# A mixture-of-experts and attention block on one core: the first expert pass split into three groups of batches instead of two

## Chip, core and metric

One NeuronCore of a Trainium2 chip (trn2) runs the whole kernel. Times are device microseconds of an execution; lower is better.

## What is computed

The input is `x` of shape (4, 1024, 128): four batches of 1024 tokens. The output is three residual steps in a row, all in float32:

```python
x = x + 0.5 * ffn(layernorm(x))
x = x + attention(layernorm(x))      # differential attention, two softmaxes per row
x = x + 0.5 * ffn(layernorm(x))

def ffn(t):                          # top 2 of 8 experts
    logits = t @ Wr.T + br
    top_v, top_i = top_k(logits, 2);  w = softmax(top_v)
    o_e = relu(t @ W1[e].T + b1[e]) @ W2[e].T + b2[e]       # 128 -> 512 -> 128
    return layer_norm(t + sum_k w_k * o_{top_i[k]}) * gamma + beta
```

## The kernel before

Each engine runs one instruction stream written out by hand, and semaphores order them. The work comes in five stages: a prologue, the first expert pass, attention over the four batches, the second expert pass, and an end.

**Prologue.** The four batches of `x` are loaded and normalised. For each batch TensorE turns the rows (`turn_rows`) and multiplies them by the router (`logits`); VectorE reads the logits and picks two experts for each token (`read_logits`, `choose`), TensorE counts (`prefix`), and VectorE works out for every token and choice a row number in a table of rows in DRAM (`place`). The three are called `route`. GpSimd then sends the normalised rows there by indirect transfers (`scatter`), 16 a batch of 128 rows each, so that the rows of one expert lie together. Between the routes TensorE turns the weights of the eight experts (`weights`), with VectorE and ScalarE copying them out of PSUM, and at the end the product of the attention's projections (`M`) is formed.

**Groups and tiles.** Batches 0 and 1 are group 0, batches 2 and 3 are group 1. When a group is placed, VectorE makes its table (`table`): the running row counts per expert (`carry`) tell how many tiles of 128 rows each expert has, and which expert and rows each tile takes. A group of two batches has 2 x 2048 / 128 + 7 = 39 tiles (`GSLOTS`), since each of eight experts may end in a tile that is not full; a pass has 78 (`SLOTS`). SyncE writes padding behind the rows of each expert (`pad`, eight a group) and waits in `group_ready` for the table, the pads and the row transfers of the group. Then it loads one tile after another into a ring of 16 buffers (`load`).

**A tile.** In `step` TensorE transposes the rows of tile s + 2 (`turn_x`, L946), multiplies tile s + 1 by the first weights (`first`, L953) and tile s by the second (`second`, L963). ScalarE copies and applies the first half of the relu, VectorE the rest (L1357) and adds the last bias (`add_b2`, L1365). In the first pass SyncE writes the result y back to DRAM (`write_y`, L357), 12 iterations behind its loads in group 0 and 7 behind in group 1. In the same loop GpSimd sends the rows of batches 2 and 3, one transfer a tile, in steps 0 to 31. From step `GATHER_AT` = 40 on it gathers the results of batches 0 and 1 (L478), and VectorE merges them into `x` in small pieces (`MERGE_AT` = 49, `MERGING`). The normalised `xn` of batch 0 is turned at steps `XN_AT` = 74 and 77. SyncE issues the pads of group 1 in its iterations 16 to 23.

**What follows.** Attention begins when the pass is over. During attention the results of batches 2 and 3 are gathered, and batches 0 to 2 are routed for the second pass. In the second pass batch 3 is routed between the tiles, a few VectorE instructions a step (`CHOOSE_AT` = 11), and GpSimd sends results and rows.

The order in the prologue before: VectorE does route 0, the weights, route 1, table 0, route 2, the copy of the projections, route 3, table 1 and `Mh`/`Ml`; then the steps begin, and TensorE waits for all four batches to be placed and for both tables. GpSimd sends batches 0 and 1 back to back (L465).

Of the kernel before, what the change touches and what calls it, by code (L numbers as in the profile page):

```python
# [29 lines left out]
def macaron_kernel(nc, x_in, w_q12, w_k12, w_v, lq1, lk1, lq2, lk2, Wr, br, W1, b1, W2, b2, gamma, beta, out):  # L30
# [9 lines left out]
    GN = GB * S  # L40
    REGION = GN + P
    ROW = D + 1
    GSLOTS = 2 * GN // P + E - 1
    SLOTS = 2 * GSLOTS
# [6 lines left out]
    assert D == P and S == TB * P and F % P == 0 and SLOTS % 2 == 0 and FC % 2 == 0 and TB % QG == 0  # L51

    rows = [nc.dram_tensor(f"rows{g}", [E * REGION + P, ROW], F32).ap() for g in range(2)]
    yrows = [nc.dram_tensor(f"yrows{g}", [GSLOTS * P, D], F32).ap() for g in range(2)]
# [3 lines left out]
    with ctx:  # L58
# [45 lines left out]
        carry, base = sb("carry", E), sb("base", E)  # L104
        carry_i = sb("carry_i", 2 * E, I32)

        GT = GN // P
        tile128 = sb("tile128", GT)
        ntile, tend, onesE = sb("ntile", E), sb("tend", E, parts=1), sb("onesE", E, parts=1)
        shift = sb("shift", 2 * E)  # L110
        sidx = sb("sidx", GSLOTS, parts=1)

        block_at = sb("block_at", SLOTS, I32, parts=1)
        row_of = sb("row_of", SLOTS, I32, parts=1)
# [37 lines left out]
        cmp2 = lent_z(GSLOTS * E)  # L152
        assert at[0] <= ATT
        eidf, offf, roff = lent_z(GSLOTS), lent_z(GSLOTS), lent_z(GSLOTS)
# [35 lines left out]
        rows_sent = [sem(f"rows_sent{par}") for par in range(2)]  # L190
# [13 lines left out]
        def route_bank(a):  # L204

            return 5 if a < BATCHES and a % 2 else 7
# [21 lines left out]
        def y_at(T):  # L228

            return bank((6, 1)[T % 2], 0, D)  # L230

# [35 lines left out]
        def y_gone(T):  # L267

            r = T % RING
            return (y_written[r], sent(T, r)) if T - RING < SLOTS else (y_sent[r], sent(T, r) - sent(SLOTS, r))  # L270
# [4 lines left out]
        BETA_AT = 18  # L275
        FIND_AT = (8, GSLOTS + 1)
        GATHER_AT = GSLOTS + 1
# [4 lines left out]
        XN_AT = SLOTS - 4  # L282
        ROWS_AT = 16
        LAST_AT, LAST_BY = GSLOTS + 9, 9
# [32 lines left out]
        def _(sp):  # L317
# [13 lines left out]
            for g in range(2):  # L331
                sp.dma_start(rows[g][E * REGION:, :], padrows[:, :]).then_inc(pads_sent, 16)
# [5 lines left out]
            def group_ready(p, g):  # L338
                sp.wait_ge(table_ready, 2 * p + g + 1)
                sp.wait_ge(pads_sent, 16 * (2 + E * (2 * p + g + 1)))  # L340
                for par in range(2):
                    sp.wait_ge(rows_sent[par], 16 * PAIRS * (2 * p + g + 1))

            def load(p, s):
                T, g = SLOTS * p + s, s // GSLOTS
# [8 lines left out]
            def write_y(s):  # L354
                r = s % RING
                wait_apart(sp, (y_sb, s + 1))
                sp.dma_start(yrows[s // GSLOTS][s % GSLOTS * P:(s % GSLOTS + 1) * P, :], ys[:, r * D:(r + 1) * D]).then_inc(y_written[r], 16)  # L357

            def all_sent(g):
                for r in range(RING):  # L360
                    sp.wait_ge(y_sent[r], sent(SLOTS + GSLOTS * (g + 1), r) - sent(SLOTS, r))

            def pads(p, g):
                sp.wait_ge(counts_ready, 2 * p + g + 1)
                for e in range(E):
                    pad(g, e)
# [4 lines left out]
            for s in range(SLOTS):  # L371
                if s == RING:
                    sp.wait_ge(counts_ready, 2)
                if RING <= s < RING + E:
                    pad(1, s - RING)
                if s == GSLOTS:
                    for t in range(s - Y_BEHIND, s - Y_NEAR):
                        write_y(t)
                    group_ready(0, 1)
                load(0, s)  # L380
                if Y_BEHIND <= s < GSLOTS:
                    write_y(s - Y_BEHIND)
                if s >= GSLOTS:
                    write_y(s - Y_NEAR)
            for s in range(SLOTS - Y_NEAR, SLOTS):
# [5 lines left out]
            for s in range(SLOTS):  # L391
                if s == 30:
                    sp.wait_ge(counts_ready, 4)
                if 30 <= s < 30 + E:
                    pad(1, s - 30)
                if s == GSLOTS:
                    group_ready(1, 1)
                load(1, s)
                if s == GSLOTS + RING - 1:
# [22 lines left out]
        def _(pool):  # L422
# [14 lines left out]
            steps.then(pool.iota(sidx[:, :], [[1, GSLOTS]], base=0, channel_multiplier=0, allow_small_or_imprecise_dtypes=True))  # L437
# [21 lines left out]
            def scatter(p, b, pieces=range(2 * TB)):  # L459
# [3 lines left out]
                for i in pieces:  # L463
                    j, k = i // 2, i % 2
                    pool.indirect_dma_start(rows[b // GB], bass.IndirectOffsetOnAxis(slot_v[:, b, j, k:k + 1], 0),  # L465
                                            rows_of(p, b)[:, j, k, :], None).then_inc(rows_sent[b % 2], 16)

            def gather(b, pieces):

                for i in pieces:  # L470
# [7 lines left out]
                    pool.indirect_dma_start(z[:, i * D:(i + 1) * D], None, yrows[b // GB],  # L478
                                            bass.IndirectOffsetOnAxis(slot[:, b * PAIRS + i:b * PAIRS + i + 1], 0)).then_inc(loaded, 16)

            def all_written(g):
                for r in range(RING):
                    wait_apart(pool, (y_written[r], sent(GSLOTS * (g + 1), r)))

            def send(s):
                T = SLOTS + s
# [17 lines left out]
            for b in range(GB):  # L504
                scatter(0, b)
            for s in range(SLOTS):
# [4 lines left out]
                if s == GATHER_AT:  # L511
                    all_written(0)
                if GATHER_AT <= s < GATHER_AT + PAIRS:
                    i = s - GATHER_AT
                    gather(0, range(i, i + 1))
                if GATHER_AT + PAIRS <= s < GATHER_AT + 2 * PAIRS:
                    i = s - GATHER_AT - PAIRS
                    gather(1, range(i, i + 1))
# [3 lines left out]
            all_written(1)  # L522
# [44 lines left out]
            for s in range(SLOTS):  # L567
# [13 lines left out]
        def _(act):  # L581
# [17 lines left out]
            def make_rows(p, b, n, tiles=range(TB)):  # L599

                if p:

                    act.wait_ge(rows_sent[b % 2], 16 * PAIRS * (BATCHES // 2 + b // 2))
# [47 lines left out]
            def step(p, s):  # L651
                t = SLOTS * p + s
                if s + 2 < SLOTS:
# [3 lines left out]
                if 0 <= s + 1 < SLOTS:  # L657
# [51 lines left out]
            def attention(b, n):  # L709
# [17 lines left out]
                for i in range(TB):  # L727
                    if last and not after and i == 6:
                        copy_tgtT(a, 0)
                    if b == 0 and i == 0:  # L730
                        for r in range(RING):
                            act.wait_ge(y_written[r], sent(SLOTS, r))
# [76 lines left out]
            for b in range(BATCHES):  # L809
# [9 lines left out]
                if b:  # L819
# [7 lines left out]
            act.wait_ge(table_ready, 2)  # L827
            for s in range(-2, SLOTS):
                step(0, s)
                if MERGE_AT + 23 <= s < MERGE_AT + 27:  # L830
# [12 lines left out]
            for s in range(-2, SLOTS):  # L843
# [10 lines left out]
                if s == GSLOTS - 1:  # L854
                    act.wait_ge(table_ready, 4)
# [26 lines left out]
        def _(pe):  # L882
# [40 lines left out]
            def logits(a):  # L923
                pe.wait_ge(tgtT_sb, 2 * a + 2)
                if a >= BATCHES:
                    pe.wait_ge(slots_ready, a)
                elif a >= 2:
                    pe.wait_ge(slots_ready, a - 1)
# [39 lines left out]
            def step(p, s):  # L968
                t = SLOTS * p + s
                if s + 2 < SLOTS:  # L970
                    turn_x(t + 2)
                    w_at[s + 2] = expert_offset(PE, s + 2)
                if 0 <= s + 1 < SLOTS:
# [21 lines left out]
            def multiply_M(b):  # L995
                pe.wait_ge(xnTh_sb, b + 2)
                pe.wait_ge(xnTl_sb, b + 2)
                for m in range(4):
                    if b:
                        pe.wait_ge(p_ready, 2 * TB * b - 1 + m // 2)  # L1000
                    elif m == 1:
                        pe.wait_ge(y_sb, SLOTS)
# [100 lines left out]
            for b in range(BATCHES):  # L1103
                turned = b + 1 == BATCHES
                if b and not turned:
# [7 lines left out]
                if not turned:  # L1113
# [19 lines left out]
            for s in range(-2, SLOTS):  # L1133
                step(0, s)
                if s in (XN_AT, XN_AT + 3):
# [5 lines left out]
            pe.wait_ge(table_ready, 3)  # L1141
            for s in range(-2, SLOTS):
# [629 lines left out]
```

## Time and profile before

| | |
|---|---|
| timed runs | 677.21 us, median of 3 (676.9 to 678.15) |
| span of the profiled execution | 746.1 us (its own time is not given apart from the span) |
| TensorE, matmul | busy 595.6 us, 80% of the span |
| VectorE / ScalarE / GpSimd | 61% / 59% / 51% |
| TensorE's mean granted clock | 0.908 |

The span is from the first to the last instruction of the execution that was recorded, and it is 69 us longer than a timed run. Busy shares are means over stages that differ; the views further down are read by stage.

### The profile page before, as it was taken

The page shows a single profiled execution, that of the slowest core. Times are in us where ns is not written, and L with a number is a line of the kernel's source. Part 1 is how long each engine was busy: PE and PEld are TensorE (multiplying, and loading weights), DVE is VectorE, ACT ScalarE, POOL GpSimd, SP SyncE. Part 2 cuts the span into 40 slices and gives each one's busy share as a digit, 9 for nine tenths or more (in the row PEclk, how much of TensorE's full clock was granted, in tenths as well). Part 3 has the DMA queues.
Part 4 walks back from the last instruction along what each step waited for, and adds up shares of the span by engine and source line. Part 5 has one row for each costly group of instructions (what it writes and reads, how often), then busy time and mean ns, then how long its engine had stood idle before and what let it go on. Part 6 is the DMA issues. An engine that isn't in the chain of part 4 may idle for free.

```text
span 746.1 us, 16949 instructions
## 1 busy us (share of the span) xinstructions
PE 595.6 (80%) x4276; PEld 544.6 (73%) x4276; DVE 454.9 (61%) x1432; ACT 443.2 (59%) x1144; POOL 380.9 (51%) x475
## 2 busy tenths in 40 slices
PE   2626189999999879899898998969288479999955
PEld 1625079999998768787886897858187479999821
DVE  5527445654667788799688789655035236457636
ACT  4434056666665677678786866837054236786744
POOL 6345225541445277568324575835745645545633
PEclk9965579999999999999999999989679679999969
DMA  8412124443333111010000000212221222522042
GB/s 278 141 38 65 50 60 102 110 104 84 98 98 90 51 29 29 8 30 22 1 1 1 23 30 15 69 29 63 57 58 54 69 74 54 175 64 59 28 147 84
DMA packets 54253, 49.22 MB, mean 66 GB/s; under 512 B 9926, under 2 KB 45938, under 8 KB 53904
## 3 DMA queue, kind: packets, MB, share of 16 engines
q1 hardware_dynamic: 45312, 31.25, 15.0%
q0 software_dynamic: 8640, 16.87, 7.3%
q8 instruction: 39, 0.64, 0.4%
q14 instruction: 54, 0.44, 0.2%
q10 hardware_dynamic: 208, 0.02, 0.0%
HBM read 25.99 MB, written 23.02 MB: 66 GB/s over the span
## 4 chain that ended last, share of the span: by engine, by line
PE 51%; DVE 19%; issue 9%; another core or an unknown queue 7%; POOL 6%; ACT 6%; DMA 1%; ACTq 1%; DVEq 0%; POOLq 0%; SPq 0%
PE banks L953 17%; PE banks L963 16%; DVE nb L1607 4%; PE banks L946 3%; PE banks L1050 3%; DVE scratch L1614 2%; PE banks L885 2%; PE banks L887 2%; PE banks L886 2%; POOL zb L478 1%; POOL rs L455 1%; ACT scratch L639 1%; POOL rows L465 1%; DVE st_r L1217 1%
## 5 line engine op out<-in xcount | busy, mean ns | idle before, releaser
L963 PE MATMUL banks<-blocks,scratch 128*128 x1248 | 172.8, 283 | 24.6 <-issue 21.9
L963 PEld LDWEIGHTS banks<-blocks,scratch 128*128 128x128 f32 x1248 | 158.3, 199 | 26.8 <-issue 26.7
L953 PE MATMUL banks<-scratch 128*128 128x128 f32 x1248 | 173.4, 284 | 4.3 <-ACT scratch L639 3.0
L1357 DVE TENSOR_SCALAR scratch<-banks,blocks 128x128 f32<-128x128 f32 x312 | 95.2, 347 | 120.5 <-PE banks L953 68.8
L953 PEld LDWEIGHTS banks<-scratch 128*128 128x128 f32 x1248 | 157.9, 198 | 9.4 <-issue 9.2
L465 POOL DMA_INDIRECT rows<-rowbuf,slot x96 | 100.1, 1043 | 55.6 <-issue 48.6
L633 ACT ACTIVATE scratch<-banks 128x128 f32<-128x128 f32 x156 | 43.3, 277 | 136.0 <-PE banks L946 66.5
L489 POOL DMA_INDIRECT results<-scratch x78 | 79.2, 1015 | 77.0 <-DVE scratch L1365 45.4
L646 ACT ACTIVATE scratch<-banks,blocks 128x128 f32<-128x128 f32 x312 | 96.8, 366 | 14.3 <-remote 6.6
L721 ACT ACTIVATE scratch<-banks,nb 128x1024 f32<-128x1024 f32 x64 | 71.3, 1115 | 45.7 <-DVE nb L1607 45.1
L639 ACT ACTIVATE scratch<-blocks 128x512 f32 x156 | 97.5, 625 | 0.0
L1607 DVE TENSOR_REDUCE nb<-banks 128x1 f32<-128x1024 f32 x64 | 76.6, 1217 | 14.7 <-PE banks L887 12.9
L1365 DVE TENSOR_TENSOR scratch<-banks,blocks 128x128 f32<-128x128 f32 x156 | 45.0, 288 | 53.0 <-PE banks L963 28.7
L478 POOL DMA_INDIRECT zb<-yrows,slot x48 | 51.5, 1073 | 44.0 <-DVE scratch L1365 26.2
L1050 PE MATMUL banks<-xn,scratch 128*128 128x128 f32 x512 | 65.5, 283 | 1.8 <-ACT scratch L707 1.7
L1050 PEld LDWEIGHTS banks<-xn,scratch 128*128 128x128 f32 x512 | 62.4, 199 | 3.1 <-issue 2.4
L885 PE MATMUL banks<-xnTh,xmh 128*128 128x512 f32 x128 | 53.7, 420 | 13.3 <-ACT scratch L721 13.2
L465 POOL DMA_INDIRECT rows<-scratch,slot x32 | 30.6, 957 | 52.7 <-DVE scratch L1365 27.2
L946 PE MATMUL banks<-ident,scratch 128*128 128x128 f32 x156 | 44.4, 285 | 16.2 <-ACT scratch L633 6.8
L887 PE MATMUL banks<-xnTh,xml 128*128 128x512 f32 x128 | 50.9, 397 | 0.0
L886 PE MATMUL banks<-xnTl,xmh 128*128 128x512 f32 x128 | 50.7, 396 | 0.0
L1614 DVE SCALAR_TENSOR_TENSOR scratch<-scratch,cc 128x1024 f32<-128x1024 f32 x32 | 40.9, 1279 | 5.3 <-POOL cc L530 5.3
(210 smaller groups left out, 882.7 us busy)
## 6 DMA issues: line engine op xcount, KB each, us to landing
scratch<-rows SPq DMA_DIRECT2D x156, 64.5 KB
yrows<-scratch SPq DMA_DIRECT2D x78, 64.0 KB
rows<-padrows SPq DMA_DIRECT2D x34, 64.5 KB
x<-in_L_attn_x_dram SPq DMA_DIRECT2D x4, 512.0 KB, 5.6
scratch<-in_L_ffn_W_dram SPq DMA_DIRECT2D x1, 2048.0 KB, 19.3
rows<-rowbuf,slot POOLq DMA_INDIRECT x96
results<-scratch POOLq DMA_INDIRECT x78
zb<-results SPq DMA_DIRECT2D x1, 1024.0 KB
```

Source lines behind the costliest of these rows:

```text
L465: pool.indirect_dma_start(rows[b // GB], bass.IndirectOffsetOnAxis(slot_v[:, b, j, k:k + 1], 0), rows_of(p, b)[:, j, k, :], None).then_inc ...
L489: pool.indirect_dma_start(results, bass.IndirectOffsetOnAxis(xt_v[:, r, D:ROW].bitcast(I32), 0), ys[:, r * D:(r + 1) * D], None, bounds_ch ...
L639: act.activation(staged(T, 0, FC), blocks[:, bass.ds(at, F)], ACT.Copy).then_inc(w1_sb, 1)
L646: ins = act.activation(hT_of(T, c), hT_at(T, c), ACT.Relu, bias=blocks[:, B1_AT + c:][:, bass.ds(at, 1)], scale=1.0)
L721: act.activation(pp, banks[:, 2 * m * 512:(2 * m + 2) * 512], ACT.Exp, bias=nb[:, 2 * i + m:2 * i + m + 1], scale=1.0, accum_out=ll[:, i:i ...
L885: pe.matmul(o, ah, bh, start=True, stop=False)
L946: pe.transpose(bank(0, 0, P), xt_v[:, r, 0:D], ident[:, :]).then_inc(xT_ps, 1)
L953: ins = pe.matmul(hT_at(T, c), staged(T, c), xT_of(T), start=True, stop=True)
L963: ins = pe.matmul(y_at(T), hT_of(T, c), blocks[:, W2_AT + c * D:][:, bass.ds(at, D)], start=(c == 0), stop=(c == FC - 1))
L1050: ins = pe.matmul(bank(6, 0, D), dT[t % 2][:, k * P:(k + 1) * P], vb[:, k * D:(k + 1) * D], start=(k == 0), stop=(k == TB - 1))
L1357: ins = dve.tensor_scalar(hT_of(T, c), hT_at(T, c), blocks[:, B1_AT + c:][:, bass.ds(at, 1)], 0.0, ALU.add, ALU.max)
L1607: dve.tensor_reduce(nb[:, c], banks[:, 2 * m * 512:(2 * m + 2) * 512], AX_X, ALU.max, negate=True).then_inc(nb_ready, 1)
```

## The change

- The first pass has three groups: batch 0, batch 1, and batches 2 and 3 (`MEMBERS`). A group of one batch has 23 tiles, so the pass has 23 + 23 + 39 = 85 (`SLOTS[0]`), the second pass still 39 + 39 = 78. Every use of `GSLOTS`, `SLOTS` and `b // GB` becomes a look-up by pass and group (`START`, `TILES`, `group_of`, `group_at`, `whole_group`, `FIRST_T`). There are three row tables and three y tables in DRAM, a semaphore `rows_sent` for each batch and a `carry` for each group.
- VectorE makes table 0 right behind route 0, ahead of the weights. Batch 3 is no longer routed in the prologue: TensorE makes its logits behind the product M, VectorE chooses in steps 0 to 2 and places in steps 4 to 6, and tables 1 and 2 are made in steps 8 to 19, a piece a step.
- TensorE and ScalarE wait for a group's table when they come to its first tile, and no longer for everything ahead of the pass.
- GpSimd sends batch 0 and four transfers of batch 1 ahead of the tiles, with a pause (`rest`) behind each: two memsets of 8 columns, each waited for. The other 44 go with the tiles, five in four steps up to step 16 and one a step after it, until step 39.
- SyncE's pads for group 1 go with iterations 15 to 22, for group 2 with 38 to 45. y is written 12 iterations behind the loads in all groups; at the start of a group five writes go ahead at once and the next five iterations write none.
- `FIND_AT`, `BETA_AT` and `XN_AT` move; `GATHER_AT` stays at step 40 and `MERGE_AT` at 49.

```diff
+    MEMBERS = [[range(0, 1), range(1, 2), range(2, 4)], [range(0, 2), range(2, 4)]]
+    TILES = [[2 * TB * len(members) + E - 1 for members in groups] for groups in MEMBERS]
+    START = [[sum(tiles[:g]) for g in range(len(tiles))] for tiles in TILES]
+    SLOTS = [sum(tiles) for tiles in TILES]
...
-        BETA_AT = 18
-        FIND_AT = (8, GSLOTS + 1)
-        GATHER_AT = GSLOTS + 1
+        BETA_AT = 28
+        AHEAD, DENSE = 4, 16
+        CHOOSE_FIRST, PLACE_FIRST, TABLE_FIRST = 0, 4, 8
+        FIND_AT = (20, 24, 34, 47)
+        GATHER_AT = 40
...
+        def first_sends(s):
+            return AHEAD + min(s, DENSE) * 5 // 4 + max(s - DENSE, 0)
...
             def group_ready(p, g):
-                sp.wait_ge(table_ready, 2 * p + g + 1)
-                sp.wait_ge(pads_sent, 16 * (2 + E * (2 * p + g + 1)))
-                for par in range(2):
-                    sp.wait_ge(rows_sent[par], 16 * PAIRS * (2 * p + g + 1))
+                sp.wait_ge(table_ready, whole_group(p, g))
+                sp.wait_ge(pads_sent, 16 * (len(rows) + E * whole_group(p, g)))
+                for b in MEMBERS[p][g]:
+                    sp.wait_ge(rows_sent[b], 16 * PAIRS * (p + 1))
...
-            for s in range(SLOTS):
-                if s == RING:
-                    sp.wait_ge(counts_ready, 2)
-                if RING <= s < RING + E:
-                    pad(1, s - RING)
-                if s == GSLOTS:
+            for s in range(SLOTS[0]):
+                for g in range(1, NGROUPS[0]):
+                    e = s - (START[0][g] - E)
+                    if e == 0:
+                        sp.wait_ge(counts_ready, whole_group(0, g))
+                    if 0 <= e < E:
+                        pad(g, e)
+                if s in START[0][1:]:
                     for t in range(s - Y_BEHIND, s - Y_NEAR):
                         write_y(t)
-                    group_ready(0, 1)
+                    group_ready(0, group_at(0, s))
                 load(0, s)
-                if Y_BEHIND <= s < GSLOTS:
+                near = [at for at in START[0][1:] if at <= s < at + Y_BEHIND - Y_NEAR]
+                if s >= Y_BEHIND and not near:
                     write_y(s - Y_BEHIND)
-                if s >= GSLOTS:
-                    write_y(s - Y_NEAR)
...
-            for b in range(GB):
-                scatter(0, b)
-            for s in range(SLOTS):
+            def rest():
+                for _ in range(2):
+                    steps.then(pool.memset(idle[:, :], 0.0))
+            for i in range(PAIRS):
+                scatter(0, 0, range(i, i + 1))
+                rest()
+            for i in range(AHEAD):
+                scatter(0, 1, range(i, i + 1))
+                rest()
+            for s in range(SLOTS[0]):
                 wait_apart(pool, (y_sb, s + 1))
-                if s < 2 * PAIRS:
-                    i = s % PAIRS
-                    scatter(0, GB + s // PAIRS, range(i, i + 1))
+                for k in range(first_sends(s), min(first_sends(s + 1), 3 * PAIRS)):
+                    i = k % PAIRS
+                    scatter(0, 1 + k // PAIRS, range(i, i + 1))
...
+            logits(BATCHES - 1)
             pe.wait_ge(M_sb, 1)
-            pe.wait_ge(slots_ready, BATCHES)
-            pe.wait_ge(table_ready, 2)
-            for s in range(-2, SLOTS):
+            for s in range(-2, SLOTS[0]):
                 step(0, s)
+                if s == CHOOSE_FIRST + 3:
+                    prefix(BATCHES - 1)
...
-            for b in range(BATCHES):
+            for b in range(BATCHES - 1):
                 route(0, b)
                 if b == 0:
+                    at_once(table(0, 0))
                     small_weights()
                     weights(range(E))
-                if b == 1:
-                    at_once(table(0))
...
-            for s in range(-2, SLOTS + 1):
+            choosing, placing = choose(BATCHES - 1), place(BATCHES - 1, BATCHES - 1)
+            tabling = itertools.chain(table(0, 1), table(0, 2))
+            for s in range(-2, SLOTS[0] + 1):
                 step(0, s)
+                if s == CHOOSE_FIRST:
+                    read_logits(BATCHES - 1)
+                if CHOOSE_FIRST <= s < CHOOSE_FIRST + 3:
+                    next(choosing, None)
+                    next(choosing, None)
+                if PLACE_FIRST <= s < PLACE_FIRST + 3:
+                    next(placing, None)
+                    next(placing, None)
+                if TABLE_FIRST <= s < TABLE_FIRST + 12:
+                    next(tabling, None)
```

## Rows read from the trace of the kernel before

**Rows 1.** The page: span, and the granted clock in 40 slices.
```profile
span 746.1 us, 16949 instructions
...
PEclk9965579999999999999999999989679679999969
```

**Rows 2.** Windows: busy us (x instructions) of each engine, clock, DMA share, GB/s.
```profile
97.00:187.00 90.00, 88.49 (x766) 88.06 (x766) 45.74 (x152) 60.40 (x184) 33.53 (x35) 0.97 0.36 94
518.00:616.00 98.00, 63.24 (x430) 59.36 (x429) 29.77 (x115) 37.25 (x109) 55.79 (x57) 0.76 0.22 62
```

**Rows 3.** The chain that ended last, 30 to 90 us: start, us, what.
```profile
41.34 6.36 another core or an unknown queue
...
72.49 11.24 another core or an unknown queue
```

**Rows 4.** Timeline of GpSimd: start us, us, instruction, idle before it.
```profile
2.69 0.29 POOL L438 TENSOR_SCALAR_AFFINE_SELECT ident<-ident 128x128 f32<-128x128 f32 x1 [0.16 <-POOL sidx L437]
...
29.09 1.24 POOL L465 DMA_INDIRECT rows<-rowbuf,slot  x1 [11.11 <-issue]
...
60.79 1.19 POOL L465 DMA_INDIRECT rows<-rowbuf,slot  x1 [11.52 <-issue]
...
80.00 0.96 POOL L465 DMA_INDIRECT rows<-rowbuf,slot  x1 [0.30 <-issue]
...
146.46 0.96 POOL L465 DMA_INDIRECT rows<-scratch,slot  x1 [0.94 <-issue]
...
271.81 2.06 POOL L478 DMA_INDIRECT zb<-yrows,slot  x1 [0.17 <-issue]
...
285.51 1.08 POOL L478 DMA_INDIRECT zb<-yrows,slot  x1 [0.17 <-issue]
```

**Rows 5.** Timeline of VectorE, same columns.
```profile
29.90 0.69 DVE L1201 COPY blocks<-banks 128x512 f32<-128x512 f32 x1 [1.42 <-PE banks L907]
...
52.07 0.23 DVE L1243 TENSOR_TENSOR lg<-banks,brb 128x64 f32<-128x64 f32 x1 [3.65 <-remote]
...
59.48 0.17 DVE L1309 CAST carry_i<-carry 128x8 int32<-128x8 f32 x1
...
63.87 0.22 DVE L1243 TENSOR_TENSOR lg<-banks,brb 128x64 f32<-128x64 f32 x1
...
71.42 0.15 DVE L1206 TENSOR_TENSOR nlam<-lame 128x1 f32<-128x1 f32 x1
```

**Rows 6.** Timeline of SyncE's queue; some rows merge several issues (x).
```profile
84.19 13.49 SPq L352 DMA_DIRECT2D scratch<-rows  x13
...
110.73 0.20 SPq L336 DMA_DIRECT2D rows<-padrows  x1
...
132.44 0.02 SPq L352 DMA_DIRECT2D scratch<-rows  x1
...
159.39 3.50 SPq L357 DMA_DIRECT2D yrows<-scratch  x6
```

**Rows 7.** DMA issues: the nearest transfer with a landing, KB, us to landing.
```profile
out_dram<-x SPq DMA_DIRECT2D x4, 256.0 KB, 2.0
```

**Rows 8.** Timeline of TensorE.
```profile
39.52 1.85 PE L931 MATMUL banks<-wrT,sum_r 128*128 128x8 f32 x16
...
68.58 3.53 PE L931 MATMUL banks<-wrT,sum_r 128*128 128x8 f32 x16
...
88.41 1.17 PE L1128 MATMUL banks<-xn 128*128 128x128 f32 x4
...
96.31 0.47 PE L946 MATMUL banks<-ident,scratch 128*128 128x128 f32 x1 [6.73 <-DVE Ml L1685]
...
249.42 0.30 PE L946 MATMUL banks<-ident,scratch 128*128 128x128 f32 x1 [1.26 <-ACT scratch L633]
```

**Rows 9.** Windows, of the tile transposes (L946) alone: busy us (x count).
```profile
104.05:183.64 79.59, 11.45 (x42) 6.01 (x42) 1.00 0.38 99
554.80:571.65 16.85, 2.24 (x8) 1.19 (x9) 1.00 0.15 45
```

More of the change, by code:

```diff
@@ L50, in macaron_kernel @@
     QG = 4
-    assert D == P and S == TB * P and F % P == 0 and SLOTS % 2 == 0 and FC % 2 == 0 and TB % QG == 0
-    rows = [nc.dram_tensor(f"rows{g}", [E * REGION + P, ROW], F32).ap() for g in range(2)]
-    yrows = [nc.dram_tensor(f"yrows{g}", [GSLOTS * P, D], F32).ap() for g in range(2)]
+    assert D == P and S == TB * P and F % P == 0 and FC % 2 == 0 and TB % QG == 0
+    rows = [nc.dram_tensor(f"rows{g}", [E * REGION + P, ROW], F32).ap() for g in range(max(NGROUPS))]
+    yrows = [nc.dram_tensor(f"yrows{g}", [tiles * P, D], F32).ap() for g, tiles in enumerate(TILES[0])]
     results = nc.dram_tensor("results", [2 * N, D], F32).ap()
@@ L189, in macaron_kernel @@
         xt_loaded = [sem(f"xt_loaded{r}") for r in range(RING)]
-        rows_sent = [sem(f"rows_sent{par}") for par in range(2)]
+        rows_sent = [sem(f"rows_sent{b}") for b in range(BATCHES)]
         went_by = sem("went_by")
@@ L230, in y_at, with group_of, group_at, whole_group @@
             return bank((6, 1)[T % 2], 0, D)
+        def group_of(p, b):
+            return [b in members for members in MEMBERS[p]].index(True)
+        def group_at(p, s):
+            return sum(s >= at for at in START[p]) - 1
+        def whole_group(p, g):
+            return sum(NGROUPS[:p]) + g + 1
+        def carry_of(p, g):
+            at = (whole_group(p, g) - 1) * E
+            return carries[:, at:at + E]
         def rows_of(p, b):
@@ L330, in _ @@
             sp.wait_ge(masks_made, 1)
-            for g in range(2):
+            for g in range(len(rows)):
                 sp.dma_start(rows[g][E * REGION:, :], padrows[:, :]).then_inc(pads_sent, 16)
@@ L566, in _ @@
             scatter(1, BATCHES - 2, range(3, 6))
-            for s in range(SLOTS):
+            for s in range(SLOTS[1]):
                 send(s)
@@ L818, in _ @@
                         copy_tgtT(b + 1, i)
-                if b:
+                if b and following:
                     gap(b)
@@ L842, in _ @@
             b, a = BATCHES - 1, 2 * BATCHES - 1
-            for s in range(-2, SLOTS):
+            for s in range(-2, SLOTS[1]):
                 step(1, s)
@@ L1102, in _ @@
             logits(0)
-            for b in range(BATCHES):
-                turned = b + 1 == BATCHES
-                if b and not turned:
+            for b in range(BATCHES - 1):
+                if b:
                     for i in range(2):
@@ L1112, in _ @@
                     weights(range(E))
-                if not turned:
+                if b + 1 < BATCHES - 1:
                     logits(b + 1)
@@ L1708, in _ @@
             routing = last_route(n)
-            choosing, placing, tabling = choose(a), place(a, BATCHES - 1), table(1)
+            choosing, placing, tabling = choose(a), place(a, BATCHES - 1), table(1, 1)
             ending = [last_sums(b, n + 1 + b) for b in range(GB)]
             adding = [last_add(b) for b in range(GB)]
-            for s in range(-2, SLOTS + 1):
+            for s in range(-2, SLOTS[1] + 1):
                 step(1, s)
```

212 lines of the change are left out of this document (110 added, 102 removed).

## Prediction

> **What bounds the kernel now.** I read the page first. TensorE's granted clock is full nearly everywhere except in slices 3 to 6 of 40, the later prologue, and here and there in slices 27 to 34, the second pass [rows 1]. So between long stretches ruled by TensorE (tiles, attention) lie two weak places, and the windows view prices the second: in a clean stretch of tiles TensorE records 766 matmuls in 90 us, 8.5 in a us; in 518 to 616 us, in the second pass, 430 in 98 us at clock 0.76 [rows 2]. At the clean rate 430 take 50.5 us, so 47.5 us are lost. The chain of waits shows what kind of time the prologue loses: 6.36 and 11.24 us are put down to "an unknown queue" [rows 3]. In the second of them VectorE stands still until 83.75 although the logits that it waits for end at 72.1.
>
> GpSimd's timeline tells when this happens. Its row transfers follow one another every 1.26 us, from 29.09 to 49.27 and from 60.79 to 80.96 us [rows 4]. Both standstills begin 12 us into such a run and end 2.8 us after it (52.07 and 83.75). In the clean tiles a transfer takes 0.96 and the gap to the next 0.94, so one comes every 1.9 us, and nobody stands still. In 518 to 616 us GpSimd has 57 instructions against 35 in the clean 90 us [rows 2].
>
> Now the span against the time. The span is 746.1 us, and the profiled execution's own time is known only by it; the timed runs have a median of 677.21, 69 us less. Clean tiles have no 69 us to give. The second pass can give 47.5, and the prologue about 21, for without standstills it would run so: the weights end some 4 us earlier, batch 1 is routed by 48 us (VectorE takes 7.4 from reading the logits to the slots [rows 5]), before GpSimd is through with batch 0 at 49.3. Sixteen more transfers end at 69.8. SyncE issues the first load 3.2 us after the last transfer, as in the trace (80.96, 84.19 [rows 4, 6]); it lands some 2.0 us later, by the nearest landing [rows 7]: the tiles start at **75.2** instead of 96.3 [rows 8]. VectorE's own road (two more routes, table 1) would be ready at 74. 47.5 + 21.1 = 68.6, and 69 are to be explained. So I take it that the timed runs hardly have these standstills, and that their prologue is bound by the row transfers of batches 0 and 1, one behind the other.
>
> A rule of the Trainium skill speaks against a gain here ("NOTIFIC — the notification-queue block", 7.1 Overflow): the block that records events never loses a record inside, it holds its producers back instead. By that rule the standstills belong to the recording, the timed runs gain nothing from their removal, and the sum below stays. The same page (section 10) says that a record costs the engine nothing, which would put them into the timed runs: the second rival. No row here tells the two apart.
>
> **The change, part by part**, in terms of the timed runs, without standstills.
>
> *The start.* Now batch 0's transfers alone gate the first load. A pause is two tiny memsets, each waited for. One costs about 0.1 us and the 0.16 until the next instruction that GpSimd's waited-for iota shows, and a transfer behind arithmetic starts 0.17 us later and takes 1.08 instead of 0.96 [rows 4]. So transfer and pause take about 1.8 us. The last of 16 ends at 29.09 + 15 x 1.8 + 1.08 = 57.2, and the first load lands at 57.2 + 3.2 + 2.0 = 62.4. Bounds of the spacing are 1.65 (no slower transfer) and 2.7 (every one like the one of 2.06 us [rows 4]): 60 to 76 us.
>
> The other road is VectorE's and TensorE's. VectorE was free for the weights 1.42 us before the copy at 29.90, at 28.5. Now table 0 comes first. Before it took 4.4 us (59.48 to 63.87 [rows 5]) for 39 tiles; for 23 I take 3.8, so 32.3. The first copy slips by 2.4 us, the end of the weights by some 2, to 39. Logits 1 take 1.85 us at the full clock, route 1 takes 7.4 from 41, and ScalarE's exponential for it lies behind the rows of batch 2, about 1.5: 50.0. Logits 2 take 3.53 us at the half clock [rows 8] and are ready at 50.5; route 2 ends at 58.0. Lambda and the copy of the projections take 1.1 (71.42 to 72.49 [rows 3, 5]), their product 1.2: 60.3. Behind it TensorE now does logits 3, 3.53 us at the half clock: **64.0**. Route 3, table 1 and batch 1's transfers are gone from this road. The later of both roads counts, 64.0 against 75.2: **-11.2 us**. With TensorE warm it is 61, and GpSimd's 62.4 counts (-12.8); with the widest pauses 76 (+1).
>
> *Seven more tiles*, 85 for 78. In the clean stretch 42 tile transposes lie in 79.59 us, 1.895 us a tile [rows 9]. **+13.3 us**, and nothing hides it, since TensorE has no gap there.
>
> *Batch 3 routed between tiles*: its 7.4 us on VectorE go over tiles 0 to 6, two tables over tiles 8 to 19. The second pass does just this with its last batch: 8 transposes in 16.85 us there, where 8 clean ones take 15.16, so 1.7 us [rows 9]. The choosing falls into the first, slow tiles: **+1.5**, between 0.5 and 3.4 (twice what the row shows).
>
> *SyncE's queue at the borders.* Iterations 15 to 22 each issue a pad, and iteration 15 waits for counts that VectorE now makes in its step 8; behind it stand loads 15 and on, and the writes of y. An iteration with a pad takes (132.44 - 110.73) / 8 = 2.71 us, a load alone 1.04, a write 0.58 [rows 6]; TensorE eats a tile in 1.9. From step 8 SyncE needs 8 x 2.71 and five writes before load 23, 25.2 us with its waits, and the load lands at 27.2; TensorE wants it 12.4 tiles behind, at 23.6. So it stands for 3.5 us. At border 46 the pads make SyncE late again (between the borders it regains only 0.27 us an iteration), and the last row transfer goes seven tiles ahead instead of eight: 2.7 by the same reckoning. Against it: with SyncE 15% quicker than in the recorded execution both vanish (18.4 + 2.5 + 2.4 is below 23.6). Bounds 0 and 6.2; I take **+3**.
>
> *The rest.* Gathers and merging keep their step numbers while the last tiles come seven later, so the pieces of xn no longer meet the merging. Where they met, tile 76 waited 1.26 us for ScalarE [rows 8]; I take **-1**, between 0, if ScalarE is late there for another reason, and -2.5. The gathers of batches 0 and 1 start at step 40 as before, those of 2 and 3 in attention as before. The new waits of the second pass ask for transfers long done; semaphores, carries and buffers per group lie on no road.
>
> Sum: -11.2 + 13.3 + 1.5 + 3 - 1 = **+5.6 us**, on the median **682.8 us**. The span of 746.1 would besides lose the prologue's 21.
>
> **The rivals.**
>
> 1. *Borders free, TensorE warm*: -12.8 + 13.3 + 0.5 - 1 = 0, so 677. For it: SyncE's iteration is not far over a tile. Against it: the half clock from 45 us on [rows 1]. Chance 0.17.
> 2. *The standstills are in the timed runs too*, the other sign. The pauses bring the transfers to 1.8 us, near the 1.9 at which nobody stands still, and the 21.1 us come on top: 661.7. Half of it: 672. Against it stands the account above: with 21 real us the rest of the trace would have to give 69 and has 48. Five or six real us are possible, and the change gains from 5.6 on. Chance 0.24, mostly near 672.
> 3. *The pauses are dear*: above a spacing of 1.9 us batch 0's transfers decide the start, and each further 0.1 costs 1.5 us; at 2.3 the time is 688. The transfer of 2.06 us speaks for it, the one of 1.08 against. Chance 0.07.
> 4. The forecast, 682.8, with its own range 678.5 to 687: chance 0.52.
>
> **The numbers.** Some 0.2% (1.35 us) can be told from no change. Faster: rival 2 and a part of rival 1, 0.28. Same: most of rival 1, 0.14. Slower: forecast and rival 3, 0.58. The range leaves out the full form of rival 2 and the far end of rival 3: 668 to 689.
>
> **What would show it.** In the profile after: 163 tile transposes; the first near 64 us; batch 0's transfers every 1.8 us and no standstill among them; TensorE waiting near tiles 21 and 44 for loads, SyncE late by its pads. The span should fall by some 15 us while the timed runs don't. A first tile at 64 and timed runs near 665 would prove me wrong on what the standstills are; free borders would take 3 us from the sum.

## The result, and the profile after

The kernel after takes 701.04 us (median of four runs, 700.69 to 703.43), the kernel before beside it 677.68 (676.9 to 679.45): ratio 1.0349, 95% interval 1.0327 to 1.0372, so 23.4 us slower. The forecast was 682.8 us, its range ended at 689. The direction was right, the size a quarter of what came.

The page of after, span and granted clock in 40 slices, to be read against [rows 1]:
```profile
span 701.6 us, 17576 instructions
...
PEclk9975899999999999999999999998999998999969
```
The recorded span falls by 44.5 us while the timed runs rise by 23.4. The weak clock of slices 27 to 34 is gone, and with it the standstills of the second pass, although nothing of that pass was changed but its waits. The window of [rows 2] in after, and then in a second recording of before that is told of below:
```profile
518.00:616.00 98.00, 90.98 (x768) 89.06 (x769) 52.01 (x183) 62.60 (x188) 73.18 (x75) 0.97 0.38 105
518.00:616.00 98.00, 91.09 (x781) 89.69 (x780) 54.63 (x186) 64.95 (x200) 67.38 (x68) 0.97 0.36 105
```
768 matmuls and 75 instructions of GpSimd stand there in after instead of 430 and 57. So the trace of before wasn't typical of its timed runs, and a clean one was made: the kernel before, unchanged, was run and recorded again (run e0). Its page, and one line each of its GpSimd, SyncE and TensorE timelines at the start:
```profile
span 675.5 us, 16949 instructions
...
PEclk9975699999999999999999999997999997999969
```
```profile
69.31 0.96 POOL L465 DMA_INDIRECT rows<-rowbuf,slot  x1 [0.31 <-issue]
```
```profile
72.89 2.59 SPq L352 DMA_DIRECT2D scratch<-rows  x3
```
```profile
75.13 0.45 PE L946 MATMUL banks<-ident,scratch 128*128 128x128 f32 x1 [7.62 <-DMA scratch<-rows]
```
The last row transfer of batches 0 and 1 ends at 70.3, the first load is issued at 72.9 and its landing starts the tiles at 75.13; the prediction had worked out 69.8, 73 and 75.2 for the timed runs. Everything below is read against this trace.

**The start of after.** TensorE, ScalarE and VectorE, one fence each:
```profile
63.71 1.19 PE L1172 MATMUL banks<-xn 128*128 128x128 f32 x4 [4.43 <-DVE xn L1726]
64.70 3.42 PE L974 MATMUL banks<-wrT,sum_r 128*128 128x8 f32 x16
67.97 0.45 PE L989 MATMUL banks<-ident,scratch 128*128 128x128 f32 x1
```
```profile
51.69 0.17 ACT L869 ACTIVATE lame<-banks 128x2 f32<-128x2 f32 x1 [3.99 <-PE banks L1162]
51.76 3.17 ACT L637 ACTIVATE scratch<-x,nm,rs 128x128 f32<-128x128 f32 x8
...
59.06 0.20 ACT L669 ACTIVATE ex<-ex 128x8 f32<-128x8 f32 x1
```
```profile
59.30 0.17 DVE L1315 TENSOR_SCALAR den<-ex 128x8 f32<-128x8 f32 x1 [3.91 <-ACT ex L669]
```
SyncE issues the first loads long before, so they decide nothing:
```profile
55.92 13.49 SPq L381 DMA_DIRECT2D scratch<-rows  x13
```
The road is the one forecast (routes, projections, product, logits 3), but the first tile comes at 67.97 instead of 64.0. ScalarE first waits 3.99 us with lambda's exponential at the head of its queue, then makes the rows of batch 3, and only then takes the exponential of route 2; VectorE stands 3.91 us for it. In before the same order cost nothing, since there the first tile waits 7.62 us for its load (the line at 75.13 above), behind the row transfers.

**The borders.** SyncE's waits and its queue, and the windows of the tile transposes (L989) over eight tiles at border 23 and six at border 46:
```profile
SPq L364 <- DVE carry_i L1356: 10.2, 1, 10.2
```
```profile
80.66 0.33 SPq L388 DMA_DIRECT2D yrows<-scratch  x1
91.88 0.35 SPq L365 DMA_DIRECT2D rows<-padrows  x1
93.06 0.34 SPq L381 DMA_DIRECT2D scratch<-rows  x1
93.52 0.37 SPq L388 DMA_DIRECT2D yrows<-scratch  x1
94.65 0.34 SPq L365 DMA_DIRECT2D rows<-padrows  x1
...
112.24 0.34 SPq L365 DMA_DIRECT2D rows<-padrows  x1
113.39 0.34 SPq L381 DMA_DIRECT2D scratch<-rows  x1
113.85 3.42 SPq L388 DMA_DIRECT2D yrows<-scratch  x6
118.19 6.55 SPq L381 DMA_DIRECT2D scratch<-rows  x6
```
```profile
102.39:126.31 23.92, 2.64 (x8) 1.21 (x9) 0.93 0.41 101
156.64:173.57 16.93, 1.89 (x6) 0.84 (x7) 1.00 0.44 106
```
SyncE stands 10.2 us for the counts of group 1, from 81 to 91.9, with the loads from tile 15 on behind them. Then come eight iterations with a pad (first and last pad 20.36 us apart, 2.91 each on average; six of the seven take 2.73 to 2.77, one 3.92) and five writes of y more, and load 23 is issued at 118.2. At [rows 9]'s 1.895 us the eight tiles take 15.16 and the six 11.37: **8.8** and **5.6 us** are lost, 14.3 in all, where the forecast had 3. Two more recordings of the unchanged kernel after (runs e9 and e14 below) lose 13.4 and 11.8 by the same tiles, so a part of this varies from run to run.

**The account** of the two clean traces. Start: 67.97 - 75.13 = -7.16. First pass, from its first to its last tile transpose: 180.41 us with 84 intervals against 150.16 with 77, +30.25, of it 7 x 1.895 = 13.3 for the tiles, 14.3 for the borders, some 1.5 for the routing at tiles 5 to 14, and 1.1 left over. Behind it (attention 0.9, second pass 0.4, end 1.7) +3.0. Sum 26.1 us, which is 701.6 - 675.5. The recorded execution is the slowest of the four; by the medians it is 23.4, so some 2.7 us of this account aren't in the typical run. The recording of e14, in the fastest run of its four, shows where they lie: its tiles start at 66.31, its borders lose 11.8, and its span is 695.9.

### The profile page after: what moved, and what is told of

Its sections match the earlier page's. It is cut to its first block, busy times and chain, and to the rows that moved or that the text cites. A ratio compares the mean times of both kernels' runs of the same rounds, so it can differ in the third digit from the quotient of the medians.

```text
span 701.6 us, 17576 instructions
## 1 busy us (share of the span) xinstructions
PE 603.5 (86%) x4395; PEld 552.5 (79%) x4395; DVE 462.0 (66%) x1464; ACT 453.9 (65%) x1172; POOL 384.3 (55%) x515
## 4 chain that ended last, share of the span: by engine, by line
PE 51%; DVE 17%; issue 9%; ACT 8%; POOL 6%; DMA 4%; SPq 3%; ACTq 0%; DVEq 0%; POOLq 0%
PE banks L996 18%; PE banks L1006 17%; DVE nb L1654 4%; PE banks L1095 3%; DVE scratch L1661 2%; PE banks L989 2%; PE banks L974 2%; PE banks L928 2%; PE banks L930 2%; PE banks L929 2%; POOL zb L512 2%; DMA scratch<-rows 1%; POOL rs L489 1%; ACT scratch L637 1%; POOL rows L499 1%
## 5 line engine op out<-in xcount | busy, mean ns | idle before, releaser
L996 PE MATMUL banks<-scratch 128*128 128x128 f32 x1304 | 179.0, 281 | 3.6 <-ACT scratch L681 1.4
L1006 PE MATMUL banks<-blocks,scratch 128*128 x1304 | 176.0, 278 | 2.4 <-issue 1.2
L1404 DVE TENSOR_SCALAR scratch<-banks,blocks 128x128 f32<-128x128 f32 x326 | 99.4, 346 | 113.2 <-PE banks L996 101.3
L996 PEld LDWEIGHTS banks<-scratch 128*128 128x128 f32 x1304 | 162.4, 196 | 8.3 <-issue 7.8
L1006 PEld LDWEIGHTS banks<-blocks,scratch 128*128 128x128 f32 x1304 | 161.2, 194 | 4.8 <-issue 4.7
L675 ACT ACTIVATE scratch<-banks 128x128 f32<-128x128 f32 x163 | 45.2, 277 | 114.2 <-PE banks L989 110.0
L688 ACT ACTIVATE scratch<-banks,blocks 128x128 f32<-128x128 f32 x326 | 101.2, 365 | 3.8 <-PE banks L996 2.4
L681 ACT ACTIVATE scratch<-blocks 128x512 f32 x163 | 101.6, 623 | 0.1
L1412 DVE TENSOR_TENSOR scratch<-banks,blocks 128x128 f32<-128x128 f32 x163 | 47.0, 288 | 26.5 <-PE banks L1006 14.6
L989 PE MATMUL banks<-ident,scratch 128*128 128x128 f32 x163 | 46.4, 284 | 14.8 <-issue 6.9
```

Of the source, the lines that this page charges most:

```text
L681: act.activation(staged(T, 0, FC), blocks[:, bass.ds(at, F)], ACT.Copy).then_inc(w1_sb, 1)
L688: ins = act.activation(hT_of(T, c), hT_at(T, c), ACT.Relu, bias=blocks[:, B1_AT + c:][:, bass.ds(at, 1)], scale=1.0)
L996: ins = pe.matmul(hT_at(T, c), staged(T, c), xT_of(T), start=True, stop=True)
L1006: ins = pe.matmul(y_at(T), hT_of(T, c), blocks[:, W2_AT + c * D:][:, bass.ds(at, D)], start=(c == 0), stop=(c == FC - 1))
L1404: ins = dve.tensor_scalar(hT_of(T, c), hT_at(T, c), blocks[:, B1_AT + c:][:, bass.ds(at, 1)], 0.0, ALU.add, ALU.max)
```

## The experiments

The kernels are called by the numbers of their runs: the fourth is e4, the eleventh e11. Runs that were sent together share the runs of before, and each ratio is to these, with its 95% interval behind it.

**Before again, and with pauses.** e0 is before unchanged. e1 adds to before, behind each of its 32 row transfers of the prologue, the pause of after:
```
 for b in range(GB):
-    scatter(0, b)
+    for i in range(PAIRS):
+        scatter(0, b, range(i, i + 1))
+        rest()
```


> The kernel before, unchanged, for a second profile. The profile on hand has standstills of 21 us in the prologue and 47 us in the second pass, and its span is 69 us over the timed runs. Theory A (the standstills belong to that one recording, and the first tile of a timed run comes at 75 us, when 32 transfers have been sent one behind the other): a profile without them shows the first tile transpose at 75, the first pass in 158 us and the second in about 155. Theory B (the start of the timed runs is nearer to 65 us): the first transpose at 65 and the second pass in 165 us as in the profile after the change. If the standstills come with this kernel in every profile, the span is again near 746 and the timed runs 677. Time 677 in all cases.

> The kernel before with the two waited-for memsets behind each of the 32 row transfers of the prologue. The pause costs 0.27 us a transfer (1.53 for 1.26 us in the profile after), 8.5 us over 32. Theory A: no standstill in a timed run to remove, and the transfers bound the start, so 677 + 8.5 = 685.5. Rival (the timed runs have standstills in the prologue and the pauses remove them): below 677. Rival (transfers don't bound the start): 677.

Before again: 677.9 us, ratio 0.9988 (0.9966 to 1.001), span 675.5, no standstill. With pauses: 687.5, ratio 1.0138 (1.0096 to 1.0179), first tile transpose at 82.92, that is 7.8 us later, near the 8.6 that 32 pauses of 0.27 us add up to. Here the pauses cost their own time and give nothing back.

**After without pauses.** Both calls of rest() are taken out.

> The kernel after without the pauses. The last transfer of batch 0 then ends at 49.3 instead of 52 us, and the first tile transpose of the profile after (68.0) waits for the logits of batch 3 on TensorE (64.9 to 68.1), not for a load. Theory A: 701, within 1 us. Rival (dense transfers slow the routing in timed runs as well): 706 or more, up to 720.

698.64 us, ratio 1.0302 (1.026 to 1.0343), 2.4 below after, with overlapping intervals; first tile transpose at 66.31 instead of 67.97, both borders still late. The earlier start isn't the pauses' doing: after with its pauses started at 66.31 too when it was recorded again (e14), and took 699.05 us there. The pauses are no large part of the 23 us.

**After with the counts of group 1 early.** The first piece of table 1, which hands SyncE the counts, comes ahead of the tiles instead of in step 8:
```
 tabling = itertools.chain(table(0, 1), table(0, 2))
+next(tabling)
 for s in range(-2, SLOTS[0] + 1):
```


> The kernel after with the first piece of table 1 (the counts for which SyncE's pads of group 1 wait) ahead of the tiles. In the profile after, SyncE waits 10.2 us for it, and tiles 18 to 25 take 8.8 us more than eight clean ones. Theory (the border at 23 is late because SyncE is held by the counts): the 8.8 us go, 692, and border 46 (5.6 us) stays. Rival (the pads themselves are too slow for a border at 23, counts or not): at most 2 to 3 us go, 698.

689.05 us, ratio 1.0152 (1.0122 to 1.0182): 12.0 us faster than after. The first pad goes out at 79.98 instead of 91.88, and SyncE has no wait for these counts left:
```profile
79.98 0.35 SPq L365 DMA_DIRECT2D rows<-padrows  x1
```
The same windows, set by the same tiles, read:
```profile
100.86:116.34 15.48, 2.18 (x8) 1.15 (x9) 1.00 0.47 117
146.68:160.09 13.41, 1.66 (x6) 0.85 (x7) 1.00 0.47 115
```
Border 23 costs 0.3 instead of 8.8, border 46 2.0 instead of 5.6, though nothing was changed there: by this pair 3.6 of its 5.6 us were SyncE's lateness handed on from border 23 (against the 4.6 of e14 it is 2.6). It issues the same pads, loads and writes, so what made border 23 dear is the wait in the queue, not the number of transfers.

**An occasion with standstills.** Four kernels went out together next. The fourth, fifth and sixth are after with the counts early, as e3. The fourth besides moves ScalarE's exponential of lambda behind that of route 2; the fifth adds to it, drops the pauses and issues the pads of group 2 eight iterations earlier; the sixth is the fifth with a copy of VectorE's moved into its wait; the seventh is before with three more empty tiles in each group:
```
-if b == 1:
+if b == 2:
     act.wait_ge(lam_ps, 1)
     act.activation(lame[:, :], bank(3, 2 * D, 2 * D + 2), ACT.Exp).then_inc(lam_exp, 1)
...
-e = s - (START[0][g] - E)
+e = s - (START[0][g] - E - 8 * (g - 1))
...
 read_logits(b)
 at_once(choose(b))
+if b == 2:
+    dve.wait_ge(qkT_ps, 1)
+    dve.tensor_copy(qkwT[:, :], bank(4)).then_inc(qkT_sb, 1)
 at_once(place(b, b))
...
-GSLOTS = 2 * GN // P + E - 1
+GSLOTS = 2 * GN // P + E - 1 + 3
```


> The kernel after with counts_ready of group 1 given before the tiles, as in the third experiment (689.05 us), and one move more: ScalarE's exponential for lambda, for which ScalarE waited 3.99 us ahead of the rows of batch 3, goes behind the exponential of route 2. Theory C (the start is 4 us later than forecast because ScalarE comes late to route 2's exponential: VectorE idle 4.1 us at den in the trace of the third experiment): rows of batch 3 start at 46 instead of 50, the exponential ends at 54.4 instead of 57.5, the first tile transpose comes at 63.1 instead of 66.2, and the time is 689.05 - 3.1 = 686.0. Rival D (something else bounds the start just behind it: the loads, which land near 60.3, or TensorE's turns of batch 3's rows ahead of prefix 2): the first transpose stays above 65 and the time within 1 us of 689.

> The fourth kernel without the pauses and with the pads of group 2 eight iterations earlier (iterations 30 to 37 instead of 38 to 45). If the 3.49 and 2.34 us intervals at tiles 46 and 47 (2.0 us over clean ones) come from SyncE being behind through the pads right before the border, they go: -2.0. The pauses cost 2.4 in the kernel after, so -2.4: 686.0 - 4.4 = 681.6. If the border waits for row transfers or counts of group 2 instead, tiles 46 and 47 keep their 2 us: 683.6.

> The fifth kernel with VectorE's copy of the turned projections moved into its wait for route 2's exponential, so that TensorE multiplies them before route 2 ends and logits 3 follow at once. Theory C: VectorE's copy, TensorE's product and its hand-over (61.0 to 63.2 us in the third experiment) leave the road: first tile transpose about 1.9 us earlier than in the fifth kernel, 61.2, time 679.7. Against before (677.2 to 678.7) this says that the change with its side costs mended only comes near break-even: start -14, seven tiles +13.3, routing +1.5. Rival: the loads of the first tiles land at 55 to 60 and bound nothing, but logits 3 wait for VectorE's slots of route 2 and the gain is under 1 us: 680.7 or more.

> The kernel before with three more (empty) tiles in each group of each pass, 84 for 78 in each pass, 12 in all; everything else keeps its place relative to the groups. If a tile costs its clean interval of 1.895 us: +22.7 us, 678 + 22.7 = 700.7. If empty tiles are cheaper or hidden behind the borders' and the last routing's waits: below +19. If more tiles also make the transfers and merges worse: above +26.

The times forecast could not be met, because before itself now took 742.8 us in all its 13 runs (740.9 to 745.4), its spans 1.7 to 1.9 us below. The four took 741.75 (ratio 0.998, 0.9953 to 1.0007), 755.6 (1.0164, 1.0132 to 1.0196), 754.5 (1.0148, 1.0107 to 1.0189) and 770.7 (1.038, 1.0344 to 1.0415). The granted clock of the fourth (with pauses), and then of the fifth (without):
```profile
PEclk9966999999999999999999999989579779999977
```
```profile
PEclk9965799999999999999999999989779689999969
```
Both have the weak second pass of [rows 1]. VectorE in the fifth, during its row transfers, and then TensorE's first tile in the fourth and in the fifth:
```profile
41.30 0.69 DVE L1241 COPY blocks<-banks 128x512 f32<-128x512 f32 x1 [4.36 <-remote]
46.30 0.69 DVE L1241 COPY blocks<-banks 128x512 f32<-128x512 f32 x1 [4.31 <-remote]
51.95 1.29 DVE L1241 COPY blocks<-banks 128x512 f32<-128x512 f32 x2 [4.96 <-remote]
```
```profile
64.64 0.45 PE L989 MATMUL banks<-ident,scratch 128*128 128x128 f32 x1
```
```profile
77.08 0.45 PE L987 MATMUL banks<-ident,scratch 128*128 128x128 f32 x1
```
In the fifth VectorE stands three times for 4.3 to 5.0 us beside the dense transfers (one each 1.26 us), each time released by something that the profile can't place ("remote"); in the fourth, with one each 1.53 us, the prologue has no such gap, and the tiles start 12.4 us earlier. The sixth and seventh, without pauses, have such gaps in the prologue as well (first tiles at 75.46 and 95.90). So the standstills can be in timed runs, and in the one trace with pauses those of the prologue are gone. The fourth and fifth differ by the pads too, which lie behind the start. Dense transfers alone don't make standstills: with the same 1.26 us, the recordings e0, e2 and e10, on other occasions, have none.

The fourth also tells lambda's exponential apart, being e3 with that one move, if on another occasion: VectorE's wait for the exponential of route 2 is 0.93 us there and 4.14 in e3. The first tile comes at 64.64 (forecast 63.1), in e3 at 66.23.
```profile
55.88 0.19 DVE L1315 TENSOR_SCALAR den<-ex 128x8 f32<-128x8 f32 x1 [0.93 <-ACT ex L669]
```

**Does it belong to the chip?** Before with pauses (e8) and after (e9) were run again, and with them the mended kernel: the tenth is the sixth once more, the eleventh is the tenth with the pauses put back.

> Before with the pauses of after behind its 32 row transfers, once more, because the chip of the last four runs timed the kernel before at 742.8 us with the standstills in its timed runs, and the chip of the runs ahead of them at 677.6 to 678.7 without. New theory E: whether VectorE and the others stand still behind dense row transfers belongs to the chip, not to the recording. Then on a chip of the first kind the pauses cost again (+9.4, as measured, ratio 1.014), and on a chip of the second kind (before near 743) they take the prologue's standstills away: first tile transpose near 83 instead of 96, and 742.8 - 13 = 730, ratio 0.982. Rival F: on such a chip the standstills have a cause that pauses don't touch; ratio 1.00 to 1.01.

> The kernel after, unchanged. On a chip of the first kind 701 (ratio 1.035). On a chip of the second kind theory E gives: start 68 instead of 96 (-28), seven tiles +13.3, borders +14.4, routing +1.5, second pass as before: 742.8 + 1 = 744 to 748, ratio 1.00 to 1.007. The fourth kernel, which lacks 12 us of the borders and 3.3 us of the start of after, measured 741.75 there, which would give 756 by those two runs: that is rival G, with a second cost of the borders hidden in the fourth kernel's run; ratio 1.018.

> The sixth kernel (counts early, lambda later, pads of group 2 earlier, copy in the wait, no pauses) once more. On a chip of the first kind 679.7 as forecast for it, ratio 1.00, first transpose 61.2; 683 if only the counts and the missing pauses help. On a chip of the second kind 754 again (first transpose 75.5).

> The tenth kernel with the pauses. On a chip of the first kind the pauses cost 1 to 2.4 us against the tenth: 681 to 682. On a chip of the second kind they take 12 to 13 us of standstills out of the start (the fourth kernel's first transpose came at 64.6, the fifth's and sixth's without pauses at 77.1 and 75.5): 754.5 - 13 = 741, first transpose 62 to 64.

Before was at 677.8 us (18 runs), and none of the four recordings here has standstills. Before with pauses: 687.3 (1.0125, 1.0071 to 1.0179); after: 702.5 (1.0323, 1.0256 to 1.0391). The mended kernels, forecast at 679.7 and 681 to 682: 683.9 (1.0079, 1.0054 to 1.0104) and 684.0 (1.0093, 1.0064 to 1.0122). The eleventh's road at the start, VectorE and TensorE:
```profile
54.41 0.23 DVE L1315 TENSOR_SCALAR den<-ex 128x8 f32<-128x8 f32 x1 [0.34 <-ACT ex L669]
```
```profile
57.88 3.55 PE L974 MATMUL banks<-wrT,sum_r 128*128 128x8 f32 x16 [2.10 <-DVE slot L1337]
61.28 0.45 PE L989 MATMUL banks<-ident,scratch 128*128 128x128 f32 x1
```
VectorE's wait for the exponential falls from 3.91 to 0.34 us, and the first tile comes at 61.28, in the tenth at 62.70 (forecast 61.2): with the fourth's wait of 0.93 this shows that ScalarE's order held the start up. The moved copy has a share in the earlier tile, and no pair of runs here parts the two. The pauses cost nothing there (684.0 against 683.9). Border 46 is clean in the tenth and costs 1.1 us in the eleventh, but the tiles from 37 on, beside the moved pads, now lose 1.2 us in the tenth and 1.7 in the eleventh: the pads' cost was mostly moved, which the forecast of 2.0 us saved had left out. By the eleventh's recording the start is 13.9 us ahead of before's, the first pass 18.8 us longer (13.3 for seven tiles, 3.1 at the borders and the moved pads, the rest mostly the routing) and what follows 1.8 longer: the change mended stays 6 us above before.

**Seven tiles alone, and the occasion once more.**

> Before with twelve more empty tiles (84 for 78 in each pass) once more, since its first run fell on a chip whose timed runs have standstills that vary (742.8 for before, 770.7 for this). On a chip of the first kind (before near 677.7): 12 x 1.895 = 22.7 us, 700.4, ratio 1.0335, if a tile costs its clean interval; below 697 if the borders' waits hide some of them; above 704 if empty tiles bring costs besides.

> Before with the pauses. On a chip of the first kind a third time 687 (nothing new). On a chip of the second kind (before near 743) theory E: first tile transpose near 83 instead of 96, about 730, ratio 0.982; rival F: 743 to 750, the pauses don't touch these standstills.

> The kernel after. On a chip of the first kind 701 to 702.5. On a chip of the second kind: start -28, seven tiles, borders and routing +29, so 744 to 748 and ratio 1.00 to 1.007 (theory E); 756, ratio 1.018, by the fourth kernel's run there (rival G).

This was the chip of the same number as in the runs at 742.8, and before took 678.8 us. So the theory that the standstills belong to the chip falls as well; they came with an occasion. Before with pauses 686.9 (1.0115, 1.0075 to 1.0155), after 699.05 (1.0319, 1.0265 to 1.0373). Twelve more tiles: 698.0 (1.0291, 1.0248 to 1.0334), 19.2 us and not 22.7. Its trace tells where: in the first pass six tiles more take 162.4 against 150.2 us, 2.0 each; in the second 174.0 against 164.6, 1.6 each, since at that pass's border TensorE loses 6.1 us and not the 10.7 of the clean trace of before; SyncE's wait there for row transfers, 5.9 us in that trace, is gone. A part of this comes back at other tiles. The change adds its seven to the first pass, so they cost 13 to 14 us, and 13.3 stands. What after and before with pauses would take on an occasion with standstills was not measured; no such occasion came again.

## Why the prediction was off

- **The standstills aren't in the timed runs**: right for the runs forecast; the clean trace starts its tiles at 75.13 against 75.2 worked out, and pauses added to before cost 8.8, 9.5 and 8.1 us in three tries and bring nothing. The account that led there (47.5 + 21.1 against 69) came out by some luck: against the clean trace the first one is 21.2 us later at the start and then longer by 5.8 in the first pass, 2.9 in attention and 40.7 in the second pass. The reason leaned to was not shown: the same kernel was recorded with spans of 675.5 and 746.1 us, so recording alone doesn't make standstills. The page that the prediction weighed ("NOTIFIC — the notification-queue block" of the Trainium skill, 7.1 Overflow) says that the block holds producers back rather than lose a record inside; no run here shows it at work or rules it out. Rival 2 described something that another occasion did show and that was absent on the day.
- **Start, 64.0 forecast, 67.97 measured** (-7.2 instead of -11.2; 66.31 in e14's recording). I gave ScalarE's exponential 1.5 us of delay in route 1, and in route 2 none: this step failed too. Measured: 2.0 us of VectorE's wait in route 1 and 3.91 in route 2, because lambda's exponential holds ScalarE's queue for 3.99 us ahead of the rows of batch 3. The fourth and eleventh kernels, with it moved, wait 0.93 and 0.34. The transfers with pauses came every 1.53 us, not 1.8, and decided nothing.
- **Seven tiles +13.3**: right; twelve more tiles in before give 2.0 us each in the first pass.
- **Batch 3 routed between tiles +1.5**: right; 1.4 at tiles 5 to 14, and the first four intervals take 0.5 more than in before.
- **SyncE's queue at the borders, +3 between 0 and 6.2: this step failed, and it is the largest miss.** 14.3 us came (11.8 and 13.4 in two other recordings). The mechanism was named (the counts of step 8, the pads behind them, load 23 late), its size not. At border 23 the counts came at 91.88, when TensorE was 11.6 clean tiles ahead of needing tile 23 and not 12.4, and SyncE then took 26.3 us to load 23 and not 25.2: with the landing tile 23 is 6.7 us late instead of 3.5, and tiles 24 and 25 lose 2.1 more, which wasn't in the reckoning. At border 46 the lateness of the first border was still in the queue, 3.6 of 5.6 us. And I halved my own reckoning of 6.2 on the thought that SyncE is 15% quicker in timed runs; in the recording of after, which has no standstills, an iteration with a pad takes 2.73 us at the least and 2.91 on average, no less than the 2.71 of [rows 6].
- **The rest, -1**: no gain. The recordings have 1.1 us left over in the first pass and 3.0 behind it, +4.1; by the medians it is about +1.5. The gain was to come from tile 76, and its interval is 3.3 us in before and in after alike.
- **The pauses**: 2.4 us of after at most, and no certain part of that; 0 in the mended kernel. The forecast had them hidden.

With these sizes the forecast's own sum is -7.2 + 13.3 + 1.5 + 14.3 + 4.1 = +26.0, against +26.1 between the two recordings and +23.4 between the medians. Of the 17.8 us between forecast and medians the borders have the most.

## What to carry over

A wait in a queue that issues loads costs what stands behind it: reckon from the moment at which the awaited value is made, and carry the lateness on to the next border, since a queue that regains 0.27 us an iteration, as this one does, needs more than twenty of them to make up 6. Hand such a value over at the earliest point; here one line moved gave back 12 of 23 us. When a resource that decided a stage is relieved, walk the next road with the order of every engine's queue, for a wait that was free (lambda's exponential) then sets the start. And a recorded span 69 us over the timed runs asks for a second recording before anything is explained by it.

## What the runs showed that I hadn't expected

The kernel before took 677.7 to 678.8 us (medians) on four occasions and 742.8 on another, where all of its 13 runs took 741 to 745 and the kernels sent with it 742 to 771, and the chip of that number took 678.8 later. On such an occasion engines stand still beside dense row transfers of GpSimd (one each 1.26 us); on the others the same transfers do no such harm. The one trace with two tiny memsets behind each transfer (one each 1.53 us) has no standstill in its prologue and starts 12.4 us earlier than the kernel without them. What sets such an occasion off stays open, and so does whether the kernels would stand still on it with no span recorded at all, since each of those runs has one.
